# Where pairs of exponentials are added in a convolution, attention and expert kernel: eight steps a batch moved from TensorE to GpSimd

## The reference

```python
x = conv_attention(x)            # 1x1 convolutions, softmax(v^T q), two batch norms, relu(o + x)
t = to_tokens(x)                 # (4, 1024, 256)
t = t + attn(ln(t))              # 8 heads of 32
t = t + experts(ln(t))           # 8 experts 256 -> 1024 -> 256, gelu, the 2 best of each token
```

## Time and profile before

| | us |
|---|---|
| median of 3 runs | 1321.52 |
| lowest, highest | 1319.78, 1323.84 |
| the profiled execution | 1325.95 |
| its span, first to last instruction | 1324.1 |
| busy in the span: TensorE matmul | 1149.3 |
| VectorE | 794.7 |
| ScalarE | 628.5 |
| GpSimd | 578.6 |

### The profile page before, as it was taken

The page is one execution under the profiler, slowest core; times in us unless marked ns, Lnnn a source line. Parts: engine busy times, 40 slices in busy tenths (PEclk is TensorE's granted clock), DMA queues, the critical chain, the costliest instruction groups (busy, mean ns, idle before and its releaser), DMA issues.

```text
span 1324.1 us, 29284 instructions
## 1 busy us (share of the span) xinstructions
PE 1149.3 (87%) x10343; PEld 756.3 (57%) x10343; DVE 794.7 (60%) x1425; ACT 628.5 (47%) x1129; POOL 578.6 (44%) x455
## 2 busy tenths in 40 slices
PE   3999698996679999989999998239999999999993
PEld 2454353643334444445444544139999999998772
DVE  2546546565578878868877881735555555555540
ACT  0636356462347756765676676313333333333332
POOL 1313224231348865276347617343444445444430
PEclk9989899896769999999999999769999999999996
DMA  4116653343412323232242301812333333332227
GB/s 123 48 64 207 269 163 90 116 144 97 159 32 63 78 74 74 74 90 86 50 106 76 108 29 57 322 33 34 49 49 50 49 50 50 50 52 42 42 30 261
DMA packets 99247, 120.47 MB, mean 91 GB/s; under 512 B 29401, under 2 KB 76441, under 8 KB 98489
## 3 DMA queue, kind: packets, MB, share of 16 engines
q1 hardware_dynamic: 78152, 70.29, 17.9%
q0 software_dynamic: 20544, 42.22, 14.3%
q10 hardware_dynamic: 432, 6.29, 1.2%
HBM read 72.97 MB, written 45.60 MB: 90 GB/s over the span
## 4 chain that ended last, share of the span: by engine, by line
PE 74%; DVE 8%; DMA 5%; ACT 5%; issue 4%; DVEq 2%; SPq 1%; POOL 1%; PEldq 0%; PEld 0%; ACTq 0%; POOLq 0%
PE PP L894 23%; PE PP L1242 14%; PE PP L1130 9%; PE PP L1104 8%; PE PP L966 3%; PE PP L1063 3%; PE PP L932 3%; PE PP L1114 3%; PE PP L1119 2%; DVE mxp L1447 2%; PE PP L1019 2%; ACT WB L821 1%; DVE WORK L1366 1%; PE PP L1215 1%; DMA q_lo_d<-WORK 1%
## 5 line engine op out<-in xcount | busy, mean ns | idle before, releaser
L821 ACT ACTIVATE WB<-PP 128x512 f32<-128x512 f32 x512 | 268.4, 606 | 175.5 <-PE PP L1130 175.4
L1447 DVE TENSOR_REDUCE mxp<-PP 128x2 f32<-128x1024 f32 x256 | 301.3, 1218 | 67.5 <-PE PP L1063 65.8
L866 ACT ACTIVATE WORK<-PP,b1c 128x256 f32<-128x256 f32 (+1 forms) x320 | 141.2, 449 | 260.6 <-PE PP L894 235.9
L631 POOL TENSOR_TENSOR WB<-WB 128x1024 f32<-128x1024 f32 x80 | 188.6, 2358 | 80.0 <-PE PP L1119 71.7
L894 PE MATMUL PP<-WORK,WB 128*128 128x256 f16 (+1 forms) x1920 | 207.7, 264 | 3.2 <-DVE WORK L1748 3.1
L1242 PE MATMUL PP<-WB,WORK 128*128 x1704 | 193.8, 273 | 0.0
L894 PEld LDWEIGHTS PP<-WORK,WB 128*128 x1920 | 176.5, 98 | 29.6 <-issue 4.3
L1242 PEld LDWEIGHTS PP<-WB,WORK 128*128 128x128 f16 x1704 | 164.4, 98 | 20.9 <-issue 0.4
L1130 PE MATMUL PP<-WORK 97*128 97x256 f16 x1024 | 159.9, 280 | 15.9 <-ACT WB L821 12.2
L599 POOL TENSOR_TENSOR WB<-WORK,WB 128x1024 f16<-128x1024 f32 x32 | 68.1, 2128 | 226.7 <-ACT WORK L732 226.7
L695 POOL DMA_INDIRECT res_d<-WORK,lb x71 | 116.8, 1645 | 104.2 <-DVE WORK L1775 86.3
(11 more groups left out here) (250 smaller groups left out, 1166.7 us busy)
## 6 DMA issues: line engine op xcount, KB each, us to landing
WORK<-in_L_ffn_W_dram POOLq DMA_DIRECT2D x32, 512.0 KB, 4.3
res_d<-WORK SPq DMA_DIRECT2D x8, 1024.0 KB, 4.5
late_d<-WB POOLq DMA_DIRECT2D x1, 6144.0 KB, 18.8
WB<-late_d ACTq DMA_DIRECT2D x3, 2048.0 KB, 17.7
WORK<-in_x_dram SPq DMA_DIRECT2D x8, 512.0 KB, 3.6
v_d<-WORK SPq DMA_DIRECT2D x4, 1024.0 KB, 4.7
WORK<-q_hi_d SPq DMA_DIRECT2D x16, 256.0 KB, 3.9
WORK<-v_d SPq DMA_DIRECT2D x8, 512.0 KB, 5.6
```

Source lines behind the costliest of these rows:

```text
L631: pool.tensor_tensor(PS[n % 2], PR[n % 3][:, 0], PR[n % 3][:, 1], ALU.add).then_inc(s("pair_kept"), 1)
L821: act.activation(PR[n % 3][:, c // 2, c % 2 * 2:c % 2 * 2 + 2], SCORES[m % 3] .rearrange("p (h n) -> p h n", h=2), ACT.Exp).then_inc(s("e_ ...
L866: act.activation(hid[u][:, k, 0:width], hidden_bank(k)[:, 0:width], ACT.Gelu, bias=b1c[:, bass.ds(e, 1), k], scale=1.0 / WSCALE)\
L1447: dve.tensor_reduce(mxp[:, n // 4 % 2, i, h:h + 2, k], PP[2 + h // 2][:, :].rearrange("p (h n) -> p h n", h=2), X_AXIS, ALU.max).then_inc( ...
```

## The change

One constant. The steps 13 to 20 of batches 1 to 3, those of picks, ranks and places, are no longer direct: GpSimd adds their pairs, and TensorE sums over `PS`. The eight scatter steps 21 to 28 stay direct.

```diff
-DIRECT = tuple(range(13, 29))
+DIRECT = SCATTER_AT
```

## The result

The changed kernel takes 1332.09 us (median of 6 runs, 1330.04 to 1336.54); the kernel before, beside it, 1321.24 (6 runs). The ratio is 1.0093, 95% interval 1.0070 to 1.0115: about 11 us slower by the medians, 12 by the ratio. The forecast was 16.7 us slower, within 1325 to 1350 us.

The account below looks back on a forecast made before the run. TensorE paces plain steps, with VectorE close behind and both near the limit in the changed steps. Profiled 1325.95 + 13.4 (waits) + 3.3 (clock) = 1342.7; from the 1321.5 median, + 16.7 gives about 1338 us, range 1325 to 1350.

Parts of the forecast that it names:

- TensorE's saving and what VectorE lets through: Steps 15 to 22, batches 1 to 3: cheaper sums take 10.3 us off TensorE; VectorE lets 5.4 us through.
- the walk: Batch 1 traced from 528 us, each start the latest of what it waits for; with waits, 5.2 us late.
- GpSimd's adds at no price of their own: 24 adds, 56.6 us on GpSimd, which has room; TensorE's pair waits end before they begin; price nothing.
- A VectorE operation with two inputs in SBUF waits for the add to end: VectorE's small operations, steps 14 to 20: each meeting costs the rest of the 2.36 us add.
- Rival 1: L1480, L1501, L1510, L1524: no waiting beyond about 0.2 us; time 1316; chance 0.11.
- rival 3: Meetings mostly missed, such as L1501 going ahead of add 16: 1322 to 1328 us; chance 0.12.
- Which operations: Batch 1: L1491, L1495, L1480, L1501, L1510, L1524, L1526 wait 0.1 to 2.0 us; add 13 over before L1489.
- The walk's sum, 5.2 + 3.0 + 5.2 = 13.4: Batches 1, 2 and 3 end late by 5.2, 3.0 and 5.2 us, together 13.4 us.
- the clock, 3.3: TensorE's clock can fall after stalls: bounds 0 and 9.8 us, two falls in all taken, 3.3 us.
- Rival 4: Clock falls at each stall, twice a batch, and every meeting is met: 1349 us; chance 0.08.
- Steps 21 on unchanged: Sign that the forecast is right: steps 16 to 20 longer, steps from 21 on as before.

Follow-up runs that it names:

- e1: Kernel before without GpSimd's adds in steps 13 to 20, TensorE summing over old PS contents (wrong softmax sums): 1322.01 us against 1327.30, ratio 0.9965.
- e11: Kernel before, direct sums kept, plus an unused GpSimd fill of PS in each of steps 13 to 20: 1317.52 us against 1317.73, ratio 0.9995.
- e5: Changed kernel, unaltered, run again on chip 5: 1343.66 us against 1327.08 for the kernel before, ratio 1.0123.
- e4: Changed kernel with each GpSimd add of steps 13 to 20 split into two half-size instructions: 1335.74 us against 1327.30 for the kernel before, ratio 1.0055.
- e8: Changed kernel with GpSimd pairs only for steps 13 to 17, adds starting when the exponentials are there: 1337.83 us against 1327.08 before, ratio 1.0059.
- e7: Changed kernel with GpSimd pairs only for steps 13 to 17, each add started with VectorE's reductions: 1325.12 us against 1327.08 before, ratio 0.9993.
- e3: Changed kernel with each add of steps 13 to 20 started with VectorE's reductions of the next step: 1337.11 us against 1327.30 before, ratio 1.0083.
- e6: Kernel before with GpSimd's scatters waiting for the previous step's exponentials instead of this step's sums: 1335.32 us against 1327.08, ratio 1.0070.
- e9: Kernel before with GpSimd's scatters waiting for their own step's exponentials instead of the sums: 1316.80 us against 1317.73, ratio 0.9994.
- e12: Kernel before with scatters waiting for their own step's exponentials, run once more in a later call: 1317.91 us against 1317.15, ratio 1.0000.

## Why the prediction was right, step by step

**TensorE's saving and what VectorE lets through.** Right. e1, which has the cheaper sums and no adds, gains 6.0 us in steps 14 to 22 and 0.35% (4.6 us) in all; the walk said 5.4 of a possible 10.3.

**GpSimd's adds at no price of their own.** Right for TensorE: it waits no longer for pairs. Right for the queue behind them: in the list of waits of the changed kernel no engine waits for GpSimd in the stretch. e11 shows the same from the other side, with a GpSimd instruction in the same places that costs nothing.

**A VectorE operation with two inputs in SBUF waits for the add to end.** Right, and it decided, as said. Carried over from two waits of 0.2 us beside an instruction of 0.73 to one of 2.36, "a wait to the end of the instruction" held in every meeting of the changed kernel's trace in which the add had begun first: ends 0.02 to 0.09 us after GpSimd's instruction. In steps 14 to 22 VectorE is busy 7.6, 4.3 and 8.1 us longer in the three batches; the walk's waits in batch 1 were 0.3 + 1.7 + 2.0 + 0.7 + 1.6 + 0.9 = 7.2. Rival 1 (no waiting) and rival 3 (mostly missed) are out. The Trainium skill, SBUF — State Buffer, section "Who interferes with whom", names this case, and adds that a GpSimd instruction which only writes doesn't contend with two inputs; the fill of e11 agrees (0.17 to 0.23 us beside it).

**Which operations.** Here the walk had a gap. It took it that operations with one input in SBUF go free. L1344 has one, and in the three batches took 0.69, 0.68 and 0.64 us in place of 0.17, each ending with add 13. In batch 1 that pushed L1489, which the walk had clear of everything, into add 14 (2.39 us). For it L1480 met nothing in batch 1: the stall had moved the steps on. The 1.7 us that the walk gave to L1480 were replaced by 2.2 at L1489, and the sum hardly saw it. That it came out so near is luck. The rule was to be had: the same section of the Trainium skill counts a tensor_scalar within SBUF among the operations that can take both ports, and L1344 agrees. Reductions, reciprocals and operations that read PSUM ran beside adds in their usual time (L1519 0.21, L1521 0.26 us).

**The walk's sum, 5.2 + 3.0 + 5.2 = 13.4, and the clock, 3.3.** By e5, whose chip has the same steps 23 to 30 as the profile of before: +6.4, +2.6 and +6.9, 15.9 in all, against 16.7. The windows of its single steps show the granted clock low in step 15 of batches 1 and 2, step 21 of both, and step 17 of batch 3:

```profile
534.04:538.96 4.92, 4.92 (x37) 1.96 (x36) 4.61 (x8) 2.09 (x4) 1.96 (x1) 0.54 0.02 1
...
655.09:659.34 4.25, 4.25 (x37) 1.73 (x36) 2.98 (x9) 1.85 (x5) 1.29 (x1) 0.66 0.02 1
...
776.19:779.09 2.90, 2.90 (x38) 1.40 (x37) 2.83 (x5) 2.07 (x6) 1.22 (x1) 1.00 0.00 0
...
786.59:791.63 5.04, 5.04 (x39) 2.09 (x38) 4.10 (x5) 2.50 (x5) 2.07 (x1) 0.55 0.00 0
```

Step 15 took 4.92 and 4.25 us with the lower clock and 2.90 without, so 2.0 and 1.4; step 21 took 4.57 and 4.51 with it and 4.37 without, 0.2 and 0.1; step 17 5.04 with it and 5.15 in batch 2 without. More falls than the two I took, but most of them where TensorE would have waited for VectorE anyway. Less the one of before (1.6), the clock is worth about 2.1 us, not 3.3; the waits some 13.8, not 13.4. Only the 15.9 is measured; this division of it is an estimate, since what a fall costs in one step can come back in the next. In batch 1 of the first trace step 15 took 4.08 us, 0.84 less than in e5, and step 16 took 4.21, 0.76 more than e5's 3.45. Nor do the batches agree one by one: the walk had 5.2, 3.0 and 5.2 before the clock, and e5's 6.4, 2.6 and 6.9 are 4.2, 2.7 and 6.9 without it. The mechanism was right; that the sum came within 1 us is in part luck. Rival 4 had every fall at full price; that is what it had wrong.

**"Steps 21 on unchanged."** Wrong for step 21: in e5 it takes 4.4 to 4.6 us against 3.85. Most of that is not the adds': e1, which has none, takes 4.3 to 4.4 there. TensorE comes to step 21 earlier by its cheaper sums, VectorE's reductions behind the places and gates do not, and L1072 waits 0.7 us for them in batch 1. Steps 23 on are unchanged in e5. In the first trace they are 8.9 us shorter than in the profile of before, which no part of the change explains. Why the first comparison gave 11 us and the second 16 stays open: the intervals of the two ratios just overlap.

## What to carry to other kernels

Moving work to an idle engine is free only if it doesn't share an access path with an engine near the limit. Before giving GpSimd a long instruction that reads SBUF, list VectorE's operations in the same stretch that read SBUF twice (and those like L1344 or e4's conversion, which scale or convert within SBUF): each that comes up during it waits to its end, however small it is, and everything queued behind it waits too. If the work has to go there, start it together with a long VectorE operation that doesn't contend, such as a reduction from PSUM (9 to 13 us between e8 and e7), or leave it where it was. Cutting it in two made each wait shorter and more operations wait, and half of the loss stayed (e4). And before a difference in a stretch that the change doesn't touch is explained, run both kernels once more, on a chip that is noted.

## What was not expected of the hardware

- A tensor_scalar of 8 elements with one input, all in SBUF, is held by a GpSimd add: 0.64 to 0.69 us for 0.17.
- GpSimd itself was hardly held: its adds took 2.34 to 2.37 us beside VectorE's operations. Where a VectorE operation with two inputs had begun up to 0.01 us ahead, it lost about 0.06 us: adds of 2.42 us behind L1508 (once in the changed kernel's trace, once in e5's) and 2.43 behind L1525 (three in e3's), low halves of 1.22 for 1.16.
- On chips 1 and 5, ScalarE's first exponential of a step came 0.2 to 1.0 us late while GpSimd issued indirect DMAs, and 2.8 us late behind three in a row, VectorE's reductions with it; on chips 13 and 15 not at all. It is worth 9 us here: the kernel before takes 1327 us on the one kind and 1317 to 1318 on the other.
- The kernel before has a step 15 of 4.97 us in batch 2, at the lower granted clock. Its versions with only the scatters moved have one or two of 4.8 to 5.0 us, and which ones changes from run to run (batch 1 in e6's trace, 1 and 2 in e9's, 2 and 3 in e12's); each is worth 1.5 to 1.6 us, so differences of 2 to 3 us between two single traces mean nothing.
